# A second expert layer worked by unordered pairs of experts, in groups of 128 tokens

## What is computed

```python
def _L1_ffn_ref(x, gate_w, gate_b, W1, b1, W2, b2):
    logits = xf @ gate_w + gate_b
    probs = jax.nn.softmax(logits, axis=-1)
    top2_vals, top2_idx = jax.lax.top_k(probs, 2)
    cw = jnp.zeros((N, Ee)).at[jnp.arange(N)[:, None], top2_idx].add(top2_vals)
    def step(acc, params):
        w1, bb1, w2, bb2, we = params
        h = jax.nn.gelu(xf @ w1 + bb1, approximate=False)
        y = h @ w2 + bb2
        return (acc + we[:, None] * y, None)
    out, _ = jax.lax.scan(step, jnp.zeros_like(xf), (W1, b1, W2, b2, cw.T))
...
x = x + _L1_ffn_ref(_layernorm(x, axis=-1), ...)
```

## Time and profile before

| | us |
|---|---|
| median of three runs | 976.24 |
| the profiled execution | 975.38 |
| its span, first to last instruction | 973.5 |
| layer 0: blocks, then groups | 0 to about 245, to about 443 |
| layer 1: blocks | about 476 to 702 |
| layer 1: hand-over to the groups | 702 to 732 |
| layer 1: groups | 732 to 929 |
| the end | 929 to 973.5 |
| PE / DVE / POOL / ACT busy, share of the span | 66% / 77% / 56% / 49% |

### The profile page before, as it was taken

The page is one execution under the profiler, slowest core; times in us unless marked ns, Lnnn a source line. Parts: engine busy times, 40 slices in busy tenths (PEclk is TensorE's granted clock), DMA queues, the critical chain, the costliest instruction groups (busy, mean ns, idle before and its releaser), DMA issues.

```text
span 973.5 us, 23618 instructions
## 1 busy us (share of the span) xinstructions
PE 641.5 (66%) x6081; PEld 547.3 (56%) x6082; DVE 752.1 (77%) x2881; ACT 480.3 (49%) x1065; POOL 545.7 (56%) x544
## 2 busy tenths in 40 slices
PE   3767667550999999999077768777207777777400
PEld 2656556450899999998056557655206655555300
DVE  6688898763699999999468989997526778787458
ACT  2365665420677777776046655665205655555100
POOL 0017677676276776767200665666763777777700
PEclk9875775755899999999557776777558999999655
DMA  8283333232233332326524454332333333333899
GB/s 221 61 199 107 112 93 95 69 107 77 71 88 89 88 87 82 86 82 176 140 57 120 137 146 136 88 88 66 94 90 87 105 98 102 94 104 97 226 233 285
DMA packets 168828, 111.51 MB, mean 115 GB/s; under 512 B 30306, under 2 KB 157737, under 8 KB 168776
## 3 DMA queue, kind: packets, MB, share of 16 engines
q1 hardware_dynamic: 151496, 77.04, 30.7%
q0 software_dynamic: 17280, 33.87, 10.4%
HBM read 60.32 MB, written 52.36 MB: 116 GB/s over the span
## 4 chain that ended last, share of the span: by engine, by line
PE 34%; DVE 22%; issue 19%; POOL 13%; DMA 5%; ACT 5%; SPq 1%; POOLq 1%; DVEq 0%; ACTq 0%
PE bank L607 10%; PE bank L621 9%; POOL row_buf L446 7%; POOL y_buf L454 5%; PE bank L509 4%; DVE xin L932 3%; PE bank L490 3%; DVE stat L877 3%; DVE x1w L984 3%; PE bank L506 2%; ACT xn L682 2%; PE bank L526 2%; PE bank L593 2%; DMA y_buf<-g_y,g_dst 2%; PE bank L513 2%
## 5 line engine op out<-in xcount | busy, mean ns | idle before, releaser
L446 POOL DMA_INDIRECT row_buf<-pay,slot x256 | 253.8, 992 | 245.0 <-DVE slot L1053 165.7
L454 POOL DMA_INDIRECT y_buf<-g_y,g_dst x284 | 291.6, 1027 | 137.0 <-issue 89.0
L607 PE MATMUL bank<-g_xT,w 128*128 128x256 f16 x1278 | 168.1, 278 | 0.9 <-ACT g_xT L786 0.3
L786 ACT ACTIVATE g_xT<-bank 128x512 f16<-128x512 f16 x142 | 84.8, 598 | 168.5 <-PE bank L593 164.4
L607 PEld LDWEIGHTS bank<-g_xT,w 128*128 x1278 | 118.3, 99 | 19.6 <-issue 2.1
L593 PE MATMUL bank<-ident,g_in 128*128 128x128 f16 x568 | 57.3, 225 | 83.6 <-DMA g_in<-row_buf 70.0
L793 ACT ACTIVATE xn<-bank,b_cols 128x256 f32<-128x256 f32 x216 | 86.8, 474 | 23.0 <-PE bank L607 15.9
L621 PE MATMUL bank<-w,g_h 128*128 x1260 | 84.4, 219 | 18.6 <-DVE g_y L1201 18.6
L793 ACT ACTIVATE xt<-bank,b_cols 128x256 f32<-128x256 f32 x210 | 84.5, 474 | 14.6 <-PE bank L607 11.4
L621 PEld LDWEIGHTS bank<-w,g_h 128*128 128x128 f16 x1260 | 76.0, 98 | 27.2 <-issue 25.1
L593 PEld LDWEIGHTS bank<-ident,g_in 128*128 128x128 f16 x568 | 37.0, 100 | 93.2 <-issue 73.9
(11 more groups left out here) (182 smaller groups left out, 1333.7 us busy)
## 6 DMA issues: line engine op xcount, KB each, us to landing
g_in<-row_buf SPq DMA_DIRECT2D x142, 130.0 KB
yin<-y_buf SPq DMA_DIRECT2D x24, 512.0 KB, 6.2
x_buf<-x1w SPq DMA_DIRECT2D x16, 520.0 KB, 4.6
xin<-x_buf SPq DMA_DIRECT2D x10, 520.0 KB, 4.4
y_buf<-g_y,g_dst POOLq DMA_INDIRECT x284
xin<-in_x_dram SPq DMA_DIRECT2D x8, 512.0 KB, 4.2
adj_in<-in_adj_dram SPq DMA_DIRECT2D x16, 256.0 KB, 3.2
row_buf<-pay,slot POOLq DMA_INDIRECT x256, 2.4
```

The source lines that it names most:

```text
L446: pool.indirect_dma_start(row_buf[L][:, :], bass.IndirectOffsetOnAxis(ap=slot[q][:, k, t:t + 1], axis=0), pay[q][:, t, :], None).then_inc( ...
L454: pool.indirect_dma_start(y_buf[L][:, :], bass.IndirectOffsetOnAxis(ap=g_dst[k][:, t:t + 1], axis=0), g_y[k][:, t, :], None, bounds_check= ...
L607: last = nc.tensor.matmul(dst, w[:, bass.ds(e * (2 * HID[L]) + (wp * HID[L] + c * P), P)], g_xT[q][:, xp, :], start=(m == 0), stop=(m == 2))
L786: nc.scalar.activation(g_xT[q][:, :, :], x_ps[q], ACT.Copy).then_inc(s.gT_sb, 1)
```

## The change

Layer 1's experts are worked by unordered pairs. A token has one place only, in the list of its pair {a, b}; there are 28 lists.

- Blocks: `route_pairs` adds two codes of the two experts and compares the sum with the 28 codes of the pairs (`hot_p`, 28 columns a tile); `places_pairs` gives one slot per token. `row` joins `pay` and `x1w`, and POOL scatters 8 times a block, rows of 1040 bytes (normalised token, token number, two weights, residual). The store to `x1_buf` is gone in layer 1; `x1w` may be written again once the scatter has read it.
- Groups: `NGP` = 91 groups of 128 tokens (64 full ones, 27 more for the lists' ends), up to 8 (`DEEP`) loaded ahead. Per group 2 transposes; `up` for both experts, 12 matmuls of 128 columns; four gelus of 128 columns; DVE cuts high and low parts of 512 columns; `down` for both experts, 14 matmuls of 128 columns, two of which add the second bias from two rows (`b2_row`); `finish` adds weight times result to the residual twice and computes the token's row number; POOL scatters 128 finished rows, 1 indirect DMA, into `out`. Two tables of experts are loaded per turn. The per-group pad DMAs (L368) are gone; the pads of all 28 lists are written at the start from 1040-byte rows.
- `pair_tables` replaces `group_tables` for layer 1: 16 short DVE instructions and one matmul that spreads the tables. `pair_constants` makes constants on DVE between `split_first(0)` and `groups(0)`.
- The whole end after the groups is gone.

The diff, cut to its core:

```diff
+PAIRS = NE * (NE - 1) // 2
+PG = P
+NGP = N_TOK // PG + PAIRS - 1
+CAPP = N_TOK + PG
+WIDE_W = ROW_W + X_END
+FULL_W = ROW_W + TILE_W
+DEEP = 8
...
-        x1w = [sb(f"x1w{q}", [P, TILES, TILE_W]) for q in range(2)]
-        pay = [sb(f"pay{q}", [P, TILES, ROW_W]) for q in range(2)]
+        row = [sb(f"row{q}", [P, TILES, FULL_W]) for q in range(2)]
+        pay = [t[:, :, 0:ROW_W] for t in row]
+        x1w = [t[:, :, ROW_W:FULL_W] for t in row]
...
-                    if not isinstance(n, int) or n >= 1:
+                    if L == 0 and (not isinstance(n, int) or n >= 1):
...
+                    sp.dma_start(row_buf[1].rearrange("(l c) w -> c l w", c=CAPP)[0:PG, :, :],
+                                 pad_row[:, :].unsqueeze(1).to_broadcast([P, PAIRS, WIDE_W])).then_inc(spare_out, 16)
...
+            def pair_groups():
+                s = SL[1]
+                sp.wait_ge(s.tables, 1)
+                for q in range(2):
+                    sp.wait_ge(s.scattered[q], 16 * TILES * NBLK // 2)
+                def load_group(g, k):
+                    r = sp.value_load(pair_tab[0:1, 2, bass.ds(g, 1)], min_val=0, max_val=PAIRS * CAPP - PG)
+                    sp.dma_start(p_in[k], row_buf[1][bass.ds(r, PG), :]).then_inc(s.g_loaded[k], 16)
+                for k in range(DEEP):
+                    load_group(k, k)
+                def load_next(g, k):
+                    sp.wait_ge(s.gT_ps, g + 1)
+                    sp.wait_ge(s.y_ready, g + 1)
+                    load_group(g + DEEP, k)
...
-            groups(1)
-            all_stored(1)
-            def last_x(n):
-                sp.dma_start(fin_x[n], tok3(x1_buf[1], n)).then_inc(fin_in[n], 16)
-            def last_results(n):
-                for k in range(TOP):
-                    sp.dma_start(fin_y[n % len(fin_y)][k], y_buf[1][n * BLK + k * N_TOK:(n + 1) * BLK + k * N_TOK, :].rearrange(
-                        "(t p) w -> p t w", p=P)).then_inc(fin_in[n], 16)
-            sp.wait_ge(stage_used, 4)
-            for n in range(NBLK):
-                last_x(n)
-            all_written(1)
-            for n in range(len(fin_y)):
-                last_results(n)
-            for n in range(NBLK):
-                sp.wait_ge(fin_done, n + 1)
-                sp.dma_start(tok3(out, n), fin_x[n][:, :, X_AT:X_END]).then_inc(out_st[n], 16)
-                if n + len(fin_y) < NBLK:
-                    last_results(n + len(fin_y))
...
-                        for k in range(TOP):
+                        for k in range(TOP if L == 0 else 1):
                             for t in range(TILES):
                                 pool.indirect_dma_start(
                                     row_buf[L][:, :], bass.IndirectOffsetOnAxis(ap=slot[q][:, k, t:t + 1], axis=0),
-                                    pay[q][:, t, :], None).then_inc(s.scattered[q], 16)
+                                    pay[q][:, t, :] if L == 0 else row[q][:, t, 0:WIDE_W], None).then_inc(s.scattered[q], 16)
...
+                            out[:, :], bass.IndirectOffsetOnAxis(ap=p_dst[k][:, 0:1], axis=0),
+                            p_out[k], None, bounds_check=N_TOK - 1, oob_is_err=False).then_inc(s.y_out[k], 16)
...
+                W = LISTS[L]
+                hot_v = (hot_any if L == 0 else hot_p)[:, :, :].rearrange("p t e -> p (t e)")
...
+                def to_feature_rows(k, turn):
+                    pe.wait_ge(s.g_loaded[k % DEEP], 16 * (turn + k // DEEP + 1))
+                    rows16 = p_in[k % DEEP].bitcast(F16)
+                    for hl in range(2):
+                        last = nc.tensor.transpose(x_ps[k % 2][:, hl, :], rows16[:, hl * D:(hl + 1) * D], ident16[:, :])
+                    last.then_inc(s.gT_ps, 1)
+                def experts(g, n):
+                    return [table_values(mybir.EngineType.PE, pair_tab[0:1, k, :], g, n, NE - 1) for k in range(2)]
+                def up(g, k, es):
+                    wait_past(pe, s.act_done, g - 3)
+                    pe.wait_ge(s.gT_sb, g + 1)
+                    w = w1[1][:, :, :, :].rearrange("p e a h -> p (e a h)")
+                    for m, e in enumerate(es):
+                        for c in range(NC[1]):
+                            dst = bank[k % 4][:, (m * NC[1] + c) * PG:(m * NC[1] + c + 1) * PG]
+                            for j, (wp, xp) in enumerate(((0, 0), (0, 1), (1, 0))):
+                                last = nc.tensor.matmul(dst, w[:, bass.ds(e * (2 * HID[1]) + (wp * HID[1] + c * P), P)],
+                                                        p_xT[k % 2][:, xp, :], start=(j == 0), stop=(j == 2))
+                    last.then_inc(s.h_ps, 1)
+                def down(g, k, es):
+                    w = w2[1][:, :, :, :, :].rearrange("p e c a d -> p (e c a d)")
+                    wait_past(pe, s.y_ready, g - 1)
+                    hid = p_h[k % AHEAD]
+                    pe.wait_ge(s.h_split, g + 1)
+                    for m, e in enumerate(es):
+                        dst = bank[5 + k % 2][:, m * D:(m + 1) * D]
+                        nc.tensor.matmul(dst, sh_row[:, :], b2_row[:, bass.ds(e * D, D)], start=True, stop=False)
+                        for c in range(NC[1]):
+                            for j, (wp, hp) in enumerate(((0, 0), (0, 1), (1, 0))):
+                                last = nc.tensor.matmul(dst, hid[:, hp, m * NC[1] + c, :],
+                                                        w[:, bass.ds(e * (2 * HID[1]) + (2 * c + wp) * D, D)],
+                                                        start=False, stop=(c == NC[1] - 1 and j == 2))
+                    last.then_inc(s.y_done, 1)
...
+                    ea, eb = experts(DEEP * i, n if last else n + 2)
+                    for k in range(n):
+                        g = DEEP * i + k
+                        if not last or k + 3 < n:
+                            to_feature_rows(k + 3, i)
+                        if not last or k + 2 < n:
+                            up(g + 2, k + 2, (ea[k + 2], eb[k + 2]))
+                        down(g, k, (ea[k], eb[k]))
...
+                def gelu(g, k, es):
+                    wait_past(act, s.h_split, g - 1)
+                    act.wait_ge(s.h_ps, g + 1)
+                    for m, e in enumerate(es):
+                        for c in range(NC[1]):
+                            at = m * NC[1] + c
+                            last = nc.scalar.activation(p_act[k % 2][:, at, :], bank[k % 4][:, at * PG:(at + 1) * PG], ACT.Gelu,
+                                                        bias=vec_cols[:, bass.ds(e * NC[1] + c + V_B1P, 1)], scale=1.0 / (S_X * S_W))
+                    last.then_inc(s.act_done, 1)
...
+            def pair_constants():
...
+                    wait_past(dve, s.scattered[q], 16 * TILES * turn)
...
+            def route_pairs(n, q, turn):
...
+                ch.did(V.tensor_tensor(key[:, :], r12[:, 0, :], r12[:, 1, :], ALU.add))
+                yield
+                V.tensor_tensor(hot_p[:, :, :], in_lists(pair_code[:, :]), key[:, :].unsqueeze(2).to_broadcast([P, TILES, PAIRS]),
+                                ALU.is_equal).then_inc(s.hot_ready, 1)
...
+            def places_pairs(n, q):
+                s = SL[1]
                 dve.wait_ge(s.rank_done, n + 1)
                 dve.wait_ge(s.rexp, n + 1)
-                ch.did(V.tensor_tensor(pos[:, :, :], rank_ps[L].rearrange("p (t e) -> p t e", e=NE),
-                                       base_run[L][:, :].unsqueeze(1).to_broadcast([P, TILES, NE]), ALU.add))
-                if L == 0:
-                    ch.did(V.tensor_scalar(den[:, :], rex[:, :, NE], 1.0, None, ALU.add))
-                else:
-                    ch.did(V.tensor_reduce(den[:, :], rex[:, :, 0:NE], AX_X, ALU.add))
+                ch.did(V.tensor_tensor(pos_p[:, :, :], rank_ps[1].rearrange("p (t e) -> p t e", e=PAIRS), in_lists(base_run[1][:, :]), ALU.add))
+                V.tensor_tensor(in_order[:, :, :], r12[:, 0:2, :], r12[:, 1:3, :], ALU.is_gt)
+                ch.did(V.tensor_reduce(den[:, :], rex[:, :, 0:NE], AX_X, ALU.add))
                 yield
-                V.tensor_tensor(base_run[L][:, :], base_run[L][:, :], tot_ps[L], ALU.add)
+                V.tensor_tensor(base_run[1][:, :], base_run[1][:, :], tot_ps[1], ALU.add)
+                V.tensor_tensor(pos_p[:, :, :], hot_p[:, :, :], pos_p[:, :, :], ALU.mult)
+                V.tensor_tensor(in_order[:, :, :], in_order[:, :, :], rex[:, :, NE].unsqueeze(1).to_broadcast([P, TOP, TILES]), ALU.max)
+                ch.did(V.reciprocal(den[:, :], den[:, :]))
+                yield
+                V.scalar_tensor_tensor(x1w[q][:, :, 0:TOP].rearrange("p t k -> p k t"), in_order[:, :, :], 1.0 / (S_H * S_W),
+                                       den[:, :].unsqueeze(1).to_broadcast([P, TOP, TILES]), ALU.mult, ALU.mult)
+                ch.did(V.tensor_reduce(slot_f[:, 0, :], pos_p[:, :, :], AX_X, ALU.add))
+                yield
```

(39 more changed lines are left out.)

361 lines of the change are left out of this document (265 added, 96 removed).

## The result

The changed kernel takes 1014.3 us (median of four runs, 1013.4 to 1015.0), the kernel before beside it 975.7: 1.039 times as long, 95% interval 1.038 to 1.041. The forecast was 1006.8, slower by 3.1%, in a range of 980 to 1032. The profiled execution of the changed kernel took 1013.35 us, its span 1011.5. All medians of this document leave out one execution of the last experiment, which took 1209.8 us at a mean granted clock of 0.55, where its others had 0.82.

What follows compares the result with a forecast made beforehand. POOL bounds the groups before, PE's sequencer after the change. Span 973.5 + 77 + 3 - 44.5 - 13 + 4 + 4 = 1004.0; with 1.9 around the span and 0.9 for the median, 1006.8 us, range 980 to 1032.

Steps and rivals of the forecast that it cites:

- The groups: Layer 1's pair groups: PE's sequencer binds at 2.55 us each, 232 us for 91, 274 with heads and ends against 197: +77.
- the clock: PE in layer 1's groups: lower clock behind up to 11 turn heads adds 3 us (0 to 6).
- A head: Start of each turn of groups: 3.0 us with a second table load; ten with a branch and two without, 35 us.
- The array: PE's array in layer 1's groups: 28 matmuls of 128 columns at 0.056 us, 1.57 us a group, under the sequencer's 2.55.
- Rival 2: Layer 1's groups: array paces at 81 ns a matmul, 2.27 us a group, sequencer doesn't bind; 979 us, chance 0.04.
- Rival 1: Layer 1's groups: fewer address instructions, sequencer doesn't bind, about 2.0 us a group; 921 us, faster, chance 0.12.
- Rival 3: Layer 1's groups: PE's clock stays at 0.50, array takes 3.0 us a group; 1039 us, chance 0.10.
- The end: After the last landing: the 44.5 us in which PE, ACT and POOL do nothing go, nothing takes their place: -44.5.
- The hand-over: From layer 1's last block to its groups: 8 scatters instead of 16 let PE start earlier, -13 us (-8 to -14).
- the blocks: Layer 1's blocks: net 0.5 to 0.6 us more per block, mostly on DVE's chain, +4 us over eight (0 to 6).
- The start: Start of the program: 3.73 MB of pad rows for 0.93 MB delay block 3's tokens, +4 us (0 to 7).

Runs made afterwards that it cites:

- the last experiment: Kernel with groups of 256 tokens and one table load, its bias matmul operands given 128 rows instead of 2: 934.1 us, 0.957 of the kernel before.

## Why the prediction was right

The bound was named rightly, as was the sign. The terms, in the prediction's order:

- **The groups** (+77, and +3 for the clock; measured +81.9). The mechanism is shown by runs: `up`'s addresses alone are worth 28 us, and with all addresses and loads gone the array has no pause left. Inside the term three sizes were off and offset each other, which is luck. A group takes 2.42 us and not 2.55 (-12 us over 91): 20 sequencer instructions, not 21 to 23, each at the 0.12 read from rows 7. A head costs the sequencer 4.4 us and leaves PE idle for 4.1, not 3.0 (+15 over 11): I took the second load at the price of the first (1.21 in rows 7), but behind another it takes 2.43; with one load PE's gap is down to 1.8. The clock's +3 has nothing in it in the turn read above, where the sequencer keeps its pace while the array is slow. Per turn that is 23.8 for the forecast 23.4 and 0.3 of clock.
- **The array** (1.57 us a group; 1.98 by the run with all fixed). Mis-sized by a quarter. The forecast wasn't harmed, since the sequencer stood above both. No row of before could show it: its second bias was added by DVE. Rival 2 had the array at 2.27 and as the bound; its steps of 128 rows are 56 ns here, and at 1.98 it isn't the bound.
- **Rival 1** (the sequencer doesn't bind, 921 us) is what the last of the runs with fixed addresses looks like: 928.8.
- **Rival 3** (the clock stays down) fell: the groups' stretch has 0.87. A head's low stretch is real, but it ends each time, as behind the head of rows 8; here it is 3.4 us behind the head at 825:

```profile
829.50:832.90 3.40, 3.40 (x29) 2.76 (x30) 0.59 (x2) 1.48 (x5) 0.00 (x0) 0.50 0.04 15
```

- **The end** (-44.5; measured -37.3). This is the step that failed: "Nothing takes its place". POOL's drain did, 7.2 us behind the last landing. It stood in the trace of before, 5.72 us long and hidden, so the question of what is late next would have found the term. It would not have found its size: there the drain ended at 930.7, 1.7 us behind the last landing. The span came out 7.5 us above the forecast's 1004.0. That this is so near to the drain's 7.2 is luck: the errors of the other terms (groups +1.9, hand-over -1.5, blocks +1.3, start -1.4) cancel to 0.3.
- **The hand-over** (-13; -14.5) and **the blocks** (+4; +5.3) came out near the forecast. For the hand-over the path is seen in the trace: the 8 scatters start at 711.0, have no pause of 2 us among them, and the tables and `split_first` are done (720.9) as the last scatter is (721.2). For the blocks no run tests which of the new instructions it is. A 1040-byte row costs POOL no more than one of 520, as assumed (count, busy us and mean ns in layer 1's blocks, of the changed kernel, then of the kernel before):

```profile
L485 POOL DMA_INDIRECT row_buf<-row,slot x56 | 55.4, 990 | 174.4 <-DVE slot L1266 159.4 <-issue 14.9
```

```profile
L446 POOL DMA_INDIRECT row_buf<-pay,slot x110 | 109.7, 997 | 124.3 <-DVE slot L1053 92.9 <-issue 31.4
```

- **The start** (+4; +2.6 in this profile). The size is near, the reason doesn't hold: moving the pads away gave nothing. In the twelve profiles of the changed kernel and its variants PE's first work in layer 0's groups lies between 245.1 and 250.8 us; in the two of the kernel before and its variant it is at 244.7 and 245.0. So a start is later by anything from 0 to 6 us, the 2.6 is one draw of these, and where it comes from stays open.

## What to carry to other kernels

Where operands are chosen by a register, count the sequencer's instructions per unit of work (here 0.12 us each on PE) beside the engine's own time, before groups are made smaller: smaller groups spread the same number of addresses over less work. Numbers for registers were best fetched by one load, since most of the load's price is fixed; where the array is the bound, a long gap without matmuls is paid again in the clock. When a long tail is removed, look at what ran hidden beneath it, and give an auxiliary matmul the same number of rows as its neighbours.

## What the runs showed of the hardware that I had not expected

- A matmul of 2 rows between matmuls of 128 rows: 0.15 us pass before it and 0.16 behind it until the next starts, where 0.056 is the step otherwise. Padding it to 128 rows was worth 43 us here (977.0 to 934.1). Why the array pays for the change isn't settled.
- The second of two loads into PE's registers, right behind the first, takes 2.43 us for 1.07; on ACT, which loads at the same time, both take 1.75 to 1.83. Whether the two engines' loads hinder each other wasn't tested. One load of twice the length takes 1.36 on PE and 1.02 on ACT. The Trainium skill ("Runtime: NRT & Kernel Launch", section "Instruction fetch mechanics") gives some 200 ns for each register of a TENSOR_LOAD. This trace disagrees for loads from an on-chip table: ten more values cost PE 0.29 us together, 0.03 each.
- POOL's drain at the end of the program takes 5.6 to 9.7 us in these kernels and doesn't wait for the end of the others' work: 9.35 us even in the run with half of POOL's scatters, where it was over 41 us before the span's end. Counted from the end of POOL's last indirect DMA it is 8.0 to 8.2 us in all ten profiles with one scatter for a group of layer 1, and 1.6 to 2.9 us in the four with two (the kernel before 2.9, the groups of 256 tokens 1.6). What sets it stays open.
